# Cross-attention and routed FFN on one core: context copy behind K's expansion, longer input rings, a new order of loads

## The reference

```python
x = x + xattn(layernorm(x), ctx, ctx, Wq, bq, Wk, bk, Wv, bv, Wd, bd)
x = x + ffn(layernorm(x), w_red, wg, W1, b1, W2, b2)

def xattn(q, k, v, ...):                 # 16 heads of 16 channels
    query, key, value = q @ Wq.T + bq, k @ Wk.T + bk, v @ Wv.T + bv
    query, key, value = (t.reshape(B, -1, H, D) for t in (query, key, value))
    logits = einsum('bsid,bsjd->bsij', query, key) / sqrt(D)   # 16 x 16 per token
    out = einsum('bsij,bsjd->bsid', softmax(logits), value)
    return transpose(out, (0, 2, 1, 3)).reshape(B, -1, O) @ Wd.T + bd

def ffn(x, ...):                         # 8 experts, one per token
    gates = softmax((x @ w_red) @ normalized(wg).T)
    e, score = argmax(gates), max(gates)
    return score * (gelu(x @ W1[e] + b1[e]) @ W2[e] + b2[e])
```

## Time and profile before

| what | value |
|---|---|
| median of 3 runs | 375.54 us (375.03 to 377.86) |
| the profiled execution's own time | 371.7 us |
| its span, first to last instruction | 369.9 us |
| PE, POOL busy | 91%, 77% of the span |
| mean granted PE clock | 0.978 |

### The profile page before, as it was taken

One profiled execution on the slowest core, in us unless ns is written; L12 is line 12 of the kernel. 1 busy time (PEld: TensorE's weight loads), 2 busy tenths in 40 slices (PEclk: granted clock), 3 DMA queues, 4 the chain that ended last, 5 costly groups with the idle time before them and its releaser, 6 DMA issues.

```text
span 369.9 us, 11173 instructions
## 1 busy us (share of the span) xinstructions
PE 334.9 (91%) x3755; PEld 286.7 (78%) x3755; DVE 258.9 (70%) x723; ACT 193.5 (52%) x525; POOL 284.2 (77%) x538
## 2 busy tenths in 40 slices
PE   7898699999999978887769996799999999999994
PEld 6686588888877766665647885779999999999993
DVE  6555778888888867788848656795656565656662
ACT  1002658777777758476775736513443435353531
POOL 3667969989898867877888577564777778888874
PEclk9999899999999999999878999999999999999998
DMA  7699979999899999997799012410222222222210
GB/s 236 214 280 286 258 174 252 254 261 273 257 286 259 234 242 297 305 300 195 202 383 374 32 46 72 119 61 29 71 63 73 71 63 71 66 66 74 62 48 1
DMA packets 55415, 63.87 MB, mean 173 GB/s; under 512 B 36558, under 2 KB 45919, under 8 KB 55360
## 3 DMA queue, kind: packets, MB, share of 16 engines
q1 hardware_dynamic: 50832, 52.77, 49.5%
q0 software_dynamic: 3744, 9.53, 8.7%
q10 hardware_dynamic: 784, 0.87, 0.7%
HBM read 42.00 MB, written 22.07 MB: 173 GB/s over the span
## 4 chain that ended last, share of the span: by engine, by line
PE 57%; POOL 18%; issue 10%; DVE 8%; DMA 3%; ACT 1%; DVEq 1%; SPq 0%; POOLq 0%; ACTq 0%
PE bQ L1138 16%; PE bKV L1108 8%; PE bL L1108 7%; POOL x L394 6%; PE bY L996 4%; PE bKV L940 4%; PE bKV L943 4%; PE bQ L1033 3%; POOL cat L374 3%; PE bO L963 3%; PE bL L952 3%; PE bT L1120 2%; POOL cp L357 2%; DMA r<-in_xc 2%; DMA wA<-in_wkvT 2%
## 5 line engine op out<-in xcount | busy, mean ns | idle before, releaser
L1138 PE MATMUL bQ<-w,wA 128*128 x312 | 74.3, 381 | 3.8 <-DVE r L790 3.4
L1138 PEld LDWEIGHTS bQ<-w,wA 128*128 128x128 f32 x312 | 56.2, 190 | 10.9 <-issue 4.9
L394 POOL TENSOR_TENSOR x<-ql,mask 128x1024 f32<-128x1024 f32 x32 | 60.6, 1894 | 0.5
L424 POOL DMA_INDIRECT out<-r,isc x39 | 40.7, 1045 | 16.7 <-issue 12.5
L836 ACT ACTIVATE pad<-ql 64x512 f32<-64x512 f32 x64 | 40.1, 626 | 23.6 <-DMA ql<-qkv_scr 23.2
L447 POOL DMA_INDIRECT r<-row_scr,ig x39 | 40.6, 1042 | 6.1 <-issue 2.1
L1108 PEld LDWEIGHTS bKV<-wA,r 128*128 128x128 f32 x320 | 38.5, 192 | 4.2 <-issue 2.4
L1108 PE MATMUL bKV<-wA,r 128*128 128x128 f32 x320 | 39.4, 276 | 2.4 <-DVE wA L777 1.8
L903 ACT ACTIVATE wA<-bL,r 128x128 f32<-128x128 f32 x76 | 21.7, 369 | 36.8 <-PE bL L1108 36.8
L903 ACT ACTIVATE wA<-bKV,r 128x128 f32<-128x128 f32 x80 | 22.8, 368 | 33.5 <-PE bKV L1108 33.5
L768 DVE TENSOR_SCALAR r<-w1b 128x1028 f32 x39 | 27.8, 712 | 15.5 <-issue 13.3
(11 more groups left out here) (175 smaller groups left out, 662.5 us busy)
## 6 DMA issues: line engine op xcount, KB each, us to landing
qkv_scr<-qkv SPq DMA_DIRECT2D x16, 768.0 KB, 5.9
ql<-qkv_scr SPq DMA_DIRECT2D x32, 384.0 KB, 5.6
r<-in_xc SPq DMA_DIRECT2D x15, 512.0 KB, 6.5
row_scr<-cat SPq DMA_DIRECT2D x32, 133.5 KB, 6.0
w1b<-in_W1b SPq DMA_DIRECT2D x8, 514.0 KB, 6.2
w<-in_W SPq DMA_DIRECT2D x8, 512.0 KB
xt<-in_x SPq DMA_DIRECT2D x15, 256.0 KB, 6.3
b2b<-in_b SPq DMA_DIRECT2D x4, 256.0 KB
```

The source lines that it names most:

```text
L394: eng.tensor_tensor(quarter(kx[:, z % 2, :]), spread(ql[z // 2 % 2][:, :, z % 2, 0:HD]), mask_k, ALU.mult).then_inc(S["kx"], 1)
L424: eng.indirect_dma_start(out, bass.IndirectOffsetOnAxis(ap=isc[k][:, :], axis=0), yo[k], None, bounds_check=NTOK - 1, oob_is_err=False).th ...
L1138: i_ = eng.matmul(bQ[:, 0:C], hT[b % 2][:, k, :], w2[:, bass.ds(eb * (KH * C) + k * C, C)], start=(k == 0), stop=(k == KH - 1))
```

## The change

- Rings: XR 14 to 16 blocks, XC 4 to 6 blocks, with a third semaphore for xc. Two small constant tiles move into a tile that is free then, which makes the room.
- SP's order. Prologue: the xc pair for blocks 4 and 5 is loaded at once, where the four loads for the output projection (`sync_setup_output`, 768 KB) were; these go to step 3, behind x (block 8) and xc (block 6). Step 5 loads xc for 8 and 10 and x for 10 and 12. From step 7 on both loads, x for block t + 7 and xc for block t + 5, are issued behind the two reads of `ql`; the xc load no longer stands right behind the store.
- POOL: from step 5 on the context copy stands behind K's expansion. The bias is added to x seven steps after the projection, not two (v = t - 7).
- The product that forms the router's columns of the output projection (`tensor_gate`) moves from block 1 to block 6, its copies on DVE to step 7. The three filling transposes of PE in each of steps 0 to 6 (`fill`) are gone. DVE makes the statistics of block 1 behind block 0's biases.
- Expert matrices: the first at step 18 instead of 22, the others from 22 on at the places that the one ahead had.
- Routing: the first piece goes from the end of step 27 into step 28, the second from the middle of step 28 to its end; POOL's first wait is for `gsub` of block 20 in place of that piece.

```diff
-XR = 14
-XC = 4
+XR = 16
+XC = 6
-MATRIX_AT = (22, 24, 26, 27, 28, 29, 30, 31, 32, 32, 33, 33, 34, 34, 35, 35)
+MATRIX_AT = (18, 22, 24, 26, 27, 28, 29, 30, 31, 31, 32, 32, 33, 33, 34, 34)
-PIECES = (("oh_a", 1), ("rv_a", 5), ...
+PIECES = (("gsub", R1), ("rv_a", 5), ...
@@ sync_inputs
             eng.wait_ge(S["ld_x0"], 16)
-            sync_setup_output(eng)
+            sync_xc(eng, 4)
             sync_x(eng, 4)
@@ sync_attention
                     eng.dma_start(qkv_scr[p], qkv[p % 2][:, :, :, :]).then_inc(S[f"st_q{p % 2}"], 16)
-                    sync_xc(eng, t + 3)
-                    if t < 8:
+                    if t < 4:
                         sync_x(eng, t + 5)
+                    if t == 3:
+                        sync_xc(eng, 6)
+                        sync_setup_output(eng)
+                    if t == 5:
+                        sync_xc(eng, 8)
+                        sync_x(eng, 10)
                 sync_row(eng, t - 10)
...
                                       ).then_inc(S[f"ld_q{p % 2}"], 16)
-                    if t > 8:
-                        sync_x(eng, t + 5)
+                    if t == 5:
+                        sync_xc(eng, 10)
+                        sync_x(eng, 12)
+                    if t > 6:
+                        sync_x(eng, t + 7)
+                        sync_xc(eng, t + 5)
@@ pool_attention
-                n, v, w, d, z = t + 1, t - 2, t - 8, t - 9, t - 5
+                n, v, w, d, z = t + 1, t - 7, t - 8, t - 9, t - 5
-                if t >= 0:
+                if t >= 0 and not live(z):
                     pool_context(eng, t + 1)
...
-                    if z == 1:
-                        eng.wait_ge(S["gx"], 1)
...
                                       ALU.mult).then_inc(S["kx"], 1)
+                    pool_context(eng, t + 1)
@@ vector_attention
                     vector_stats(eng, 0)
-                    vector_stats(eng, 1)
                 if t < 7:
                     vector_kv(eng, a)
                     vector_q(eng, a)
+                    if t == 0:
+                        vector_stats(eng, 1)
                     vector_stats(eng, t + 2)
-                if a == 1:
+                if a == 7:
                     eng.wait_ge(S["gx"], 1)
...
+                if t == ROUTE + 1:
+                    vector_early(eng, 0)
                 if live(a) and t >= 7:
                     vector_kv(eng, a)
...
-                if ROUTE < t < ROUTE + 7:
+                if ROUTE + 1 < t < ROUTE + 7:
                     vector_early(eng, t - ROUTE)
                 if live(a) and t >= 7:
                     vector_q(eng, a)
-                if t == ROUTE:
-                    vector_early(eng, 0)
+                if t == ROUTE + 1:
+                    vector_early(eng, 1)
@@ tensor_attention, tensor_project
-                if t < 7:
-                    fill(eng, 3, bA)
-            if a == 1:
+            if a == 6:
                 tensor_gate(eng)
```

More of the change, by code:

```diff
@@ L55 @@
 SELR = NH2 + 2
-PIECES = (("oh_a", 1), ("rv_a", 5), ("rv_a", 10), ("rv_a", 13), ("texp_a", 1), ("selk_a", 1), ("taken_a", 1))
-SEMS = ("ld_xx ld_cc ld_x0 ld_x1 ld_x2 ld_c0 ld_c1 st_q0 st_q1 ld_q0 ld_q1 st_r0 st_r1 st_r2 st_r3 st_r4 ld_wq ld_wkv ld_wd ld_wo ld_g ld_gr ld_gt ld_b ld_bd "
+PIECES = (("gsub", R1), ("rv_a", 5), ("rv_a", 10), ("rv_a", 13), ("texp_a", 1), ("selk_a", 1), ("taken_a", 1))
+SEMS = ("ld_xx ld_cc ld_x0 ld_x1 ld_x2 ld_c0 ld_c1 ld_c2 st_q0 st_q1 ld_q0 ld_q1 st_r0 st_r1 st_r2 st_r3 st_r4 ld_wq ld_wkv ld_wd ld_wo ld_g ld_gr ld_gt ld_b ld_bd "
         "ld_bc ld_w1 ld_w2 ld_b2 filled ident iotas const cp mask4 pad0 nmax gpow ctr0 ctr gmm gate gx gxs "
@@ L120, in build @@
         pad = sb("pad", [P, 3, 4 * C])
-        x0 = sb("x0", [P, 2 * NH * P])[:, :]
+        x0 = sb("x0", [P, 3744])[:, :]
         kx = x0[:, 0:2 * NG_ * NC_ * HD].rearrange("p (k n) -> p k n", k=2)
@@ L155, in build @@
         bdm = b2b[:, 5 * C:6 * C].rearrange("p (a c) -> p a c", a=KC)
+        io_r1, io_k1 = b2b[:, 6 * C:6 * C + P], b2b[:, 6 * C + P:6 * C + P + NSP]
         wgT = sb("wgT", [NG, NE])
@@ L161, in build @@
         r0 = sb("r0", [P, 3800])[:, :]
-        r1 = sb("r1", [P, 2 * W1W + C])[:, :]
+        r1 = sb("r1", [P, XC * 4 * P])[:, :]
         xcT = r1[:, 0:XC * 4 * P].rearrange("p (n a c) -> p n a c", n=XC, a=4)
@@ L256, in sync_xc @@
                     eng.wait_ge(S["qq"], c - XC + 2)
-                eng.dma_start(xcT[:, c % XC:c % XC + 2, :, :], xc[c // 2]).then_inc(S[f"ld_c{c // 2 % 2}"], 16)
+                eng.dma_start(xcT[:, c % XC:c % XC + 2, :, :], xc[c // 2]).then_inc(S[f"ld_c{c // 2 % 3}"], 16)
         def sync_inputs(eng):
@@ L352, in pool_context @@
                 else:
-                    eng.wait_ge(S[f"ld_c{a // 2 % 2}"], (a // 4 + 1) * 16)
+                    eng.wait_ge(S[f"ld_c{a // 2 % 3}"], (a // 6 + 1) * 16)
                 if a > 1:
```

2 lines of the change are left out of this document (removed).

## The result

The changed kernel takes 394.25 us (median of 6 runs, 390.34 to 395.51), the kernel before 375.38 us (6 runs, 374.24 to 377.86): 1.052 of its time, 95% interval 1.047 to 1.057. The prediction said 380.0 and a range up to 386. The profiled execution took 395.5 us, its span is 393.7, the mean PE clock 0.946. Some executions of each kernel run a few us longer at a lower granted clock; the ratios leave them out, the medians don't.

A forecast was written before the change was run, and what follows sets the result against it. The prediction took the DMA queue's store-to-reads loop, slower than PE, as the bound. Its terms moved step 36 from 195.81 to 200.0, and +4.2 on the 375.54 us median was rounded to 380, range 371 to 386.

The forecast's parts named there:

- the price of a load: Steady DMA loop: each 512 KB xc load moved behind the reads adds 0.91 us, making the loop 11.28 a pair.
- reads of pair 4: End of the prologue, step 9: SP issues these reads at 62.0 us, between 59 and 64.5, against 58.77 before.
- from there to pair 13: Steps 9 to 27: nine intervals of 11.28, plus 3.6 for four W1 loads, minus 0.5; pair 13 at 166.6.
- from there to pair 15: Two intervals without x or xc, with two W1 loads each: 23.4 us, pair 15 at 190.0.
- from there to step 36: From pair 15's reads to PE's step 36: no earlier than 10.0 us later, so 200.0 against 195.81 before.
- from step 36 to the span's end: Tail: unchanged, shifting as a whole; later W2 and b2 loads cost 0, between -0.9 and +1.8 us.
- The rival's 1.28: Rival on the steady loop: a 512 KB load costs 1.28 us at 410 GB/s, step 36 at 206.3, total 386; chance 0.13.
- 0 for what leaving the old one gives back: Gap between store and reads: its latency stays as long without the xc load, so removing the load saves 0.
- The first part: What bounds the kernel before: the DMA queue's loop, 10.37 us a pair, is slower than PE's 9.87 by 0.5.
- half-clock stretches: Prologue without fills: more PE stretches at 1.2 GHz possible, each some 1.6 us, costing nothing while the queue sets the pace.
- about 1 later: Prologue: PE's first xc wait, for blocks 6 and 7 (6.54 us to land before), ends about 1 us later.
- Pair 7 as the first with a large stall: Steady stage: 4.0 us of slack is eaten within three pairs; pair 7, expanded in step 19, stalls first, then every second step.

The follow-up runs named there:

- e13: The kernel before with an xc ring of 6 and the xc load for block t + 5 behind the reads, x as before: 387.61 us, 1.037.
- e1: The changed kernel with the steady xc load issued right behind the store again from step 7, x still behind the reads: 382.94 us, 1.017.
- e2: The changed kernel with the prologue of the kernel before up to step 7, steady stage as changed: 388.68 us, 1.036 of the kernel before.
- e3: The changed kernel with the old prologue and the steady xc load right behind the store again: 376.66 us, 1.003 of the kernel before.
- e15: The kernel before with longer rings and both steady loads behind the reads, each xc load cut to its first block (256 KB): 380.81 us, 1.017.
- e8: The kernel before with longer rings, context copy behind K's expansion, and steady xc and x loads two blocks earlier, both behind the store: 368.80 us, 0.980.
- e9: The kernel before with one edit, every x load right behind the store: 371.26 us, 0.993.
- e16: The changed kernel with the expert matrices' loads at their old steps: 394.65 us, 1.055 of the kernel before.
- e12: e1 with the fill matmuls of steps 0 to 6 back: 379.37 us, 1.012 of the kernel before.
- e11: e1 with SP's prologue loads in the old order and number, other prologue edits kept: 379.53 us, 1.014 of the kernel before.
- e5: The kernel before with longer rings, copy behind K's expansion, xc two blocks earlier behind the store, x two blocks earlier behind the reads: 375.31 us, 0.998.

## Why the prediction was wrong

The direction and the mechanism held: a load taken from behind the store and put behind the reads lengthens the DMA loop, and the latency gap stands empty. Every size was too small: the price of a load, the cost of the new prologue, and the distance from the last reads to step 36, where a lower bound stood in for a value. For the profiled execution the forecast was 371.7 + 4.2 = 375.9; it took 395.5, 19.6 more. On the medians it is 14.3 more (394.25 against 380.0): the execution profiled before was 3.7 under its median, the one profiled after 1.3 over, so some 5 of the 19.6 belong to which executions were profiled. The steps of the profiled execution:

| step of the prediction | forecast | measured | off by |
|---|---|---|---|
| reads of pair 4 | 62.0 | 68.09 | 6.1 |
| from there to pair 13 | 104.6 | 110.37 | 5.8 |
| from there to pair 15 | 23.4 | 24.23 | 0.8 |
| from there to step 36 | 10.0 | 13.34 | 3.3 |
| from step 36 to the span's end | 174.1 | 177.7 | 3.6 |

**The price of a load.** "I take 0.91 for each xc load": the steady loop was to be 11.28 a pair. The five intervals of the changed kernel without a W1 load are 11.99, 10.95, 11.90, 12.16 and 12.12, mean 11.82: 1.45 more than 10.37. e13 against the kernel before gives 1.59 with the same three W1 loads in both. The two pairs of runs that differ in xc's place alone give less, 1.15 (12.26 - 11.11, e1) and 1.14 (12.26 - 11.12, e2 and e3). So the price is 1.1 to 1.6 us, and above 0.91 in every comparison. What was wrong with 0.91 is that it was a mean over 12.01, 11.45 and 10.39, whose first two alone give 1.36; I had no reason in the trace for the third. The rival's 1.28, bytes over 410 GB/s, lies within the measured span. From 85 to 91 the changed kernel moved 316 GB/s with its engines 0.95 busy, and 524,288 bytes at that rate are 1.66; at the 231 GB/s of the loop as a whole they are 2.27. That the price falls with the bytes is what e15 says; which rate sets it is not shown. The figures that the prediction quotes from the Trainium skill ("DMA: Bandwidth & Descriptors", Anatomy of one DMA) are measured there on DMAs issued by GpSimd. The loads here are issued by SyncE, and the 1.2 us worked out from those figures lies within the measured 1.1 to 1.6.

**What the old place gives back.** "0 for what leaving the old one gives back": this fits the runs. The gap of the changed kernel is no shorter and emptier (0.00 from 91.2 to 92.3, where before 0.16 from 110.5 to 112), e1 and e3 get 1.15 and 1.14 a pair back by filling it, and e8 fills it with 768 KB.

**Who owned the loop.** The first part said that the queue's loop of 10.37 was slower than PE. This was only half true: SP waited 29.4 us for DVE ahead of its stores, a row of the view that I read and didn't use. SP's timeline of the kernel before, the stores of pairs 4, 5 and 8:

```profile
54.68 0.33 SPq L279 DMA_DIRECT2D qkv_scr<-qkv  x1
...
64.57 0.33 SPq L279 DMA_DIRECT2D qkv_scr<-qkv  x1
...
94.14 0.33 SPq L279 DMA_DIRECT2D qkv_scr<-qkv  x1
```

From 54.68 to the store at 104.01 they are 9.87 us apart, which is PE's pace. Only the reads slipped by 0.5 a pair, as the time from a store to its reads grew from 4.09 to 6.56 us. The queue fell behind, but it did not yet set the pace, and the sum treated 10.37 as the time of a closed loop. This also hid a gain: the x load in the full stretch cost the kernel before 2.8 to 4.3 us (e9), and in e9 the reads follow the store of pair 8 by 4.36 us (94.35 to 98.71), not by 6.10.

**The prologue.** Forecast for pair 4: +3.2. Measured +9.3 in the profiled execution. But its reads don't come at one time: over the executions profiled here they are issued at 58.1 to 60.8 with the old prologue, and at 68.09, 66.73 (e1) and 63.79 (e16) with the new one. e16 has the same program as the changed kernel up to step 18, and comes within 1.8 of the forecast 62.0. What differs is the granted clock. PE's wait for xc in e16, and the stretch after it:

```profile
33.22 1.10 PE L950 MATMUL bKV<-wA,r 128*128 128x256 f32 x4 [3.41 <-DMA r<-in_xc]
```

```profile
33.20:40.00 6.80, 6.33 (x63) 5.39 (x64) 2.62 (x7) 0.37 (x1) 5.17 (x10) 1.00 1.14 283
```

The clock is 1.00 there, without any fills; in e12 it falls to 0.50 (37 to 39 us) with the fills in place, and its reads of pair 4, at 65.27, lie among those without. So 4.3 of the 6.1 too much for pair 4 came with half-clock stretches, which some executions of this prologue have and others don't, and the fills' share in that is not shown. The prediction had such stretches in mind, at some 1.6 each, and booked them at nothing, "while the queue sets the pace". This doesn't cover a stage where the queue waits for PE's first blocks. The Trainium skill ("TensorE: Matmul & The Clock Gate", Part 1) says that the throttled clock is the default and that activity releases it. The trace of the changed kernel agrees (0.50 after 4.64 us idle); e16 shows no fall after 3.41.

The load order is the other part. With the old one and no fills (e11) the reads of pair 4 come at 60.93, 2.9 before e16's. xc for blocks 6 and 7 took 8.45 us, where "about 1 later" was written. The wait of 2.32 for block 1's copy was put at 1.0.

**From the reads to step 36.** 10.0 was a lower bound ("no earlier than"), and the sum used it as the value. In the kernel before this distance was 15.6 (180.23 to 195.81), so the evidence for more stood in the rows.

**The tail.** Taken as 0, measured 3.6. The steps 36 to 39 hold 1.9 of it (216.03 to 235.52 against 195.81 to 213.45), with row stores queued behind W2 loads; the rest lies behind. e16 has 177.9 there with the old W places, so these are not the cause in the changed kernel. Most variants have 176.7 to 181, so the kernel before with 174.1 is the exception; its profiled execution was a short one. Why stays open.

**What held.** Pair 7 as the first with a large stall (step 19 to 20: 7.5 us, after losses of up to 1.0 a step from step 14 on); after it the stalls come in two steps out of four (8.25 and 7.96 us, 131.75 to 147.96) and not in every second; the xc waits of POOL mostly gone, 4.2 us in all; the routing wait of the earlier trace rows gone. The copy and the longer rings with earlier loads are worth nothing by themselves (e5: 0.998).

The best version that ran is e8, the rings and the copy kept, the old prologue, and both loads right behind the store: 368.80 us, 0.980 (0.974 to 0.986) of the kernel before.

## What to carry to other kernels

Where a kernel stores to DRAM and reads back, look for room on the queue between the store's issue and the first bytes of the reads. Here 768 KB of loads fitted there. A load of 512 KB behind the reads cost 1.1 to 1.6 us a pair, and a mean over three intervals of one trace was too thin to price it. Before calling such a loop bound by the queue, look at all waits of the issuing engine, the one for the data to be stored, the one for the landing and the one for the buffer to be read into, and at the pace of the stores, not only of the reads. Before a difference between two traces is put down to an edit, look at other executions of the same part: the prologue here varied by 4 us with the granted clock. And a lower bound is not a value: when an interval is used as "no earlier than", look up how long it was.

## What the runs showed of the hardware

- What stood behind a store on its queue didn't hold up its landing, what stood ahead did. With 768 KB of loads behind the store and 768 KB of reads ahead of it (e8) the reads followed the store by 5.29 us (93.90 to 99.19); with 512 KB behind and 1 MB ahead (the kernel before) by 6.56; with no load behind and 1.5 MB ahead (the changed kernel) by 8.49.
- Moving the loads into the gap raised what the DMA engines did over many pairs: busy share 0.87 and 231 GB/s in the changed kernel (70 to 130 us), 0.97 and 263 in the kernel before (58 to 110), 1.02 and 269 in e8 (60 to 130).
- Four matmuls of 128x256 took 1.1 us at 2.4 GHz and 2.05 at 1.2 GHz after an idle stretch of 4.64. After shorter ones the first four took 1.10 (3.41 idle, no fills, e16; 3.04 idle, no fills, e11) and 1.18 (3.78 idle, fills, e12), but in e12 the next four took 1.91.
- A load of 512 KB behind the reads, not behind the store, lengthened the mean interval by 1.14 (e2 and e3), 1.15 (the changed kernel and e1) and 1.59 us (e13 and the kernel before), one of 256 KB by 0.75 (e15 and the kernel before).
